# Reading the second attention's operands during the middle stage, and the gate chain in another order

## The chip, the cores and the metric

One core of one Trainium2 chip runs the whole program. Times are microseconds of device time for one execution; the kernel before takes 1930.31 us (median of 3 runs, 1929.67 to 1931.03). The trace is of one profiled execution.

## The reference, cut to what matters

Two post-norm transformer layers over x of 2048 tokens by 128 features. Layer 0 is a causal attention of 16 heads of 64 and a gated feed-forward of width 512; layer 1 is an attention of 16 heads of 8 with a Gaussian bias on the scores, and a linear layer. What the change touches lies between the feed-forward of layer 0 and the attention of layer 1:

```python
mixed_q = x @ wq + bq;  mixed_k = x @ wk + bk;  mixed_v = x @ wv + bv
glo = mean(mixed_q, axis=1)                          # over all 2048 tokens
c = tanh(mixed_q @ wfq + bfq + (glo @ wfg + bfg))    # the gate
P = sigmoid(sum(c * up, -1)) * 2048;  Z = sigmoid(sum(c * uz, -1)) * 2048   # per head
G = -(j - P) ** 2 * 2.0 / Z ** 2                     # j: position of the key
scores = q @ k.T / sqrt(8) + G;  probs = softmax(scores);  ctx = probs @ v
```

## The kernel before, in words

The program is a row of blocks; a block ends when all its engines have reached its end. First comes attention 0 (to 879 us of the span), then the middle stage (to 1100.9 us), attention 1 (to about 1866 us), and the last products and norms.

**The middle stage** runs over four chunks (c = 0 to 3) of 512 tokens: norm 0, the feed-forward, norm 1, then the projections of layer 1's query (kind "q"), key ("k"), value ("v") and gate ("f"). A chunk's projections are worked in between the feed-forward of the next chunk, those of chunk 3 at the end, alone. All orders are written out by hand, one list for each engine: TensorE (PE), ScalarE (ACT), VectorE (DVE), GpSimd (POOL), and SyncE (SP), which issues the DMAs.

Attention 1 takes scores from one bf16 product, so q and k are split into three bf16 parts each: POOL splits q into `parts_q` (lines 955 to 961), DVE splits k into `parts_k` (1235 to 1238). SP writes them to DRAM as `q_rows` and `k_rows` (line 927), where a head has 48 rows (`R_A`): six pairings of a part of q with a part of k, of 8 features each. The bias G is a square in the key's position, so it becomes 12 more rows: six of the coefficient a, three of w1 and three of w0 (each coefficient split in three bf16 parts; a's parts stand twice). Against them stand rows of constants in `krows`.

**The gate chain** at the end of the stage is: q of chunk 3 (ACT `mq`, 1121), DVE's mean `glo`, PE's `wfg` product (1075), DVE's `cbias` (1283), ACT's tanh of all four chunks from `cpre` into `cgate` (1165), PE's 64 narrow products (1082) that sum c over a head's features with `up` and `uz` into two banks of PSUM, `ps_g0` (for P) and `ps_g1` (for Z), ACT's two sigmoids (1169), and DVE's arithmetic: reciprocal `rz` (1288), `na` (1289), `uu` (1292), `f1` (1295), `f0` (1298). ACT and DVE then split these three into `parts_a`, `parts_w1`, `parts_w0` (1172, 1175, 1305), and SP writes them to `g_rows` (line 937), a first (six DMAs), then w1 and w0 (three each). The block ends when all of it has landed.

**Attention 1** works in 16 units u: four groups of four heads, by four chunks of 512 queries. SP reads a unit's operands into one of three slots of `qrows` (`load_q`, 1407 and 1409: four copies of 48 and four of 12 rows) and a group's keys into one of two slots of `krows` (`load_k`, 1414). The first unit's operands are read at the block's start. A unit's maxima come first (PE products 1478 into `ps_x` and `ps_y`, DVE maxima 1574 and 1578, 64 blocks of 512 keys); they run a unit ahead of its scores (1514), exponentials (ACT 1453) and weighted values (1524). SP puts the maxima into `qrows` too (`place_max`, 1432), and reads unit u + 2 when the scores of unit u - 1 are done.

Of the kernel before, what the change touches and what calls it, by code (L numbers as in the profile page):

```python
# [14 lines left out]
P = 128  # L15
# [125 lines left out]
def build(nc, a, out):  # L141
# [643 lines left out]
    GR = R_M - R_A  # L785
# [5 lines left out]
    gd = nc.dram_tensor("g_rows", (GR, NC, H1, S), BF16, kind="Internal").ap()  # L791
# [3 lines left out]
    krows = l1.enter_context(nc.sbuf_tensor("krows", [P, 2, HG, HALF], BF16))  # L795

    with ExitStack() as ctx:
# [11 lines left out]
        act_b = sb("act_b", [P, NH, QC])  # L809
# [16 lines left out]
        parts = {n: sb(f"parts_{n}", [P, 3, S], BF16) for n in "qk"}  # L826
        cpre = sb("cpre", [P, S - QC])
# [6 lines left out]
        cbias = sb("cbias", [P, 1])  # L834
        sig = sb("sig", [P, 2, JB])
# [20 lines left out]
        s_bl = sem("s_bl")  # L856
        s_tp = sem("s_tp")
# [25 lines left out]
        s_dr = sem("s_dr")  # L883

# [18 lines left out]
        def _(sp):  # L903
# [19 lines left out]
            for c in range(NQ):  # L923
                for n, dst, split_done, order in (("q", qd, s_pq, Q_PART), ("k", kd, s_pk, K_PART)):
                    sp.wait_ge(split_done, c + 1)
                    for m, part in enumerate(order):
                        sp.dma_start(dst[:, D1 * m:D1 * m + D1, CHUNK[c]], parts[n][:, part, CHUNK[c]]).then_inc(s_dr, 16)
                        n_d += 1
            for n, row, rep in (("a", 0, 2), ("w1", 6, 1), ("w0", 9, 1)):
                for i in range(3):  # L930
# [4 lines left out]
                    for r in range(rep):  # L935
                        src = gparts[n][:, i] if n != "a" else gparts[n][:, i].to_broadcast([P, NC, JB])
                        sp.dma_start(gd[row + rep * i + r].rearrange("c h (j s) -> (h j) c s", s=JB), src).then_inc(s_dr, 16)
                        n_d += 1
            sp.wait_ge(s_dr, 16 * n_d)

        @block.gpsimd
        def _(pool):
# [10 lines left out]
            for c in range(NQ):  # L953
                pool.wait_ge(s_qs, c + 1)
                pool.tensor_copy(parts["q"][:, 0, CHUNK[c]], qs[:, c % 2]).then_inc(s_pd, 1)
                pool.wait_ge(s_pd, 3 * c + 1)
                pool.tensor_tensor(qs[:, c % 2], qs[:, c % 2], parts["q"][:, 0, CHUNK[c]], ALU.subtract).then_inc(s_pd, 1)
                pool.wait_ge(s_pd, 3 * c + 2)
                pool.tensor_copy(parts["q"][:, 1, CHUNK[c]], qs[:, c % 2]).then_inc(s_pd, 1)
                pool.wait_ge(s_pd, 3 * c + 3)  # L960
                pool.tensor_tensor(parts["q"][:, 2, CHUNK[c]], qs[:, c % 2], parts["q"][:, 1, CHUNK[c]], ALU.subtract)\
# [3 lines left out]
        def _(pe):  # L965
# [106 lines left out]
            for kind in "qfkv":  # L1072
                project(kind, c)
# [692 lines left out]
```

## Time and profile before

| | before |
|---|---|
| median of 3 runs | 1930.31 us |
| the profiled execution | 1929.04 us |
| its span, first to last instruction | 1927.2 us |
| PE, DVE, ACT, POOL busy, share of span | 86%, 69%, 50%, 31% |
| mean granted TensorE clock, share of 2.4 GHz | 0.957 |
| DMA, mean over the span | 20 GB/s |

The profiled execution is 1.84 us longer than its span, and 1.27 us below the median. Shares are averages over stages with different limits, so they do not tell what a change between two stages is worth; that is read from the stretch between 1060 and 1115 us. The page's own chain of what ended last covers only the last norm, so the chain here is followed engine by engine.

### The profile page before, as it was taken

Reading aid. Unit: us, or ns where it says so; the run is one execution under the profiler, and the core shown is the slowest. Engines: PE = TensorE matmul, PEld = TensorE weight load, DVE = VectorE, ACT = ScalarE, POOL = GpSimd, SP = SyncE. Lnnn points to the kernel's source line nnn. Section 1 sums busy time; section 2 is a strip of 40 time slices with the busy share of each in tenths; the row PEclk is TensorE's granted clock in tenths of the full one; section 3 lists DMA queues with packets and bytes.
Section 4 is the critical chain, followed back from the end, with each engine's and each line's share of the span. In section 5 each row is a group of like instructions: output and inputs, shape, how many; then the busy total and the mean of one; then the engine's idle time right before and its main releaser. Section 6 shows DMA issues by size and latency. Waiting matters only on the chain. (4 is left out here: it accounts for less than half of the span.)

```text
span 1927.2 us, 27492 instructions
## 1 busy us (share of the span) xinstructions
PE 1651.8 (86%) x10672; PEld 529.6 (27%) x10672; DVE 1333.2 (69%) x2289; ACT 968.9 (50%) x1116; POOL 596.4 (31%) x325
## 2 busy tenths in 40 slices
PE   7899999999999999997999358888888888888863
PEld 3233333333333333323444201111111111111121
DVE  5767676767667676743333388888888888888716
ACT  3344444444444444442443206777777777777760
POOL 1576757667676767780000000000000000000000
PEclk9999999999999999997999658999999999999995
DMA  5000000000000000001011440112111211111000
GB/s 126 1 2 1 2 1 2 2 1 2 1 2 1 2 1 2 2 1 18 14 52 33 122 71 1 28 36 37 24 22 22 38 22 22 22 22 23 2 2 25
DMA packets 58420, 39.04 MB, mean 20 GB/s; under 512 B 20238, under 2 KB 55602, under 8 KB 58290
## 3 DMA queue, kind: packets, MB, share of 16 engines
q1 hardware_dynamic: 57474, 37.08, 9.2%
q8 instruction: 85, 1.39, 0.3%
q14 instruction: 45, 0.37, 0.1%
q10 hardware_dynamic: 816, 0.20, 0.0%
HBM read 25.53 MB, written 10.49 MB: 19 GB/s over the span
## 5 line engine op out<-in xcount | busy, mean ns | idle before, releaser
L1453 ACT ACTIVATE probs<-ps_e 128x1024 f32<-128x1024 f32 x512 | 498.6, 1022 | 256.1 <-PE ps_e L1514 254.7
L393 POOL TENSOR_TENSOR acc<-acc,probs 128x1024 f32<-128x1024 f32 (+3 forms) x256 | 502.7, 1964 | 210.2 <-DVE probs L754 139.0
L424 ACT ACTIVATE probs<-ps_e 128x1024 f32<-128x1024 f32 (+1 forms) x320 | 288.4, 901 | 375.1 <-PE ps_e L563 242.5
L1574 DVE TENSOR_REDUCE maxpart<-ps_x 128x2 f32<-128x1024 f32 x351 | 428.1, 1220 | 68.0 <-PE ps_x L1478 65.2
L582 PE MATMUL ps_o<-probs,v 128*64 128x512 f32 (+3 forms) x1280 | 307.6, 558 | 14.1 <-DVE probs L754 11.1
L1524 PE MATMUL ps_o<-probs,v 128*9 128x512 f32 x2048 | 269.2, 598 | 46.1 <-ACT probs L1453 30.4
L674 DVE TENSOR_REDUCE maxpart<-ps_x 128x2 f32<-128x1024 f32 x192 | 233.9, 1218 | 56.8 <-PE ps_x L492 54.0
L1478 PE MATMUL ps_x<-krows,qrows 60*128 60x512 bf16 x702 | 152.7, 402 | 102.2 <-DVE maxpart L1574 70.6
L1578 DVE TENSOR_REDUCE maxpart<-ps_y 128x1 f32<-128x512 f32 x322 | 220.4, 684 | 18.8 <-PE ps_y L1478 15.9
L1514 PE MATMUL ps_e<-qrows,krows 62*128 62x512 bf16 x1024 | 220.1, 383 | 10.2 <-DMA qrows<-maxrow 5.9
L677 DVE CUSTOM_DVE_ANT_0 masked<-ps_x,later 128x128 f32<-128x128 f32 (+3 forms) x256 | 115.2, 487 | 65.2 <-PE ps_x L492 64.0
L1478 PE MATMUL ps_y<-krows,qrows 60*128 60x512 bf16 x322 | 129.2, 401 | 7.8
L492 PE MATMUL ps_x<-k_hi,q_hi 64*128 64x512 f16 (+3 forms) x640 | 112.2, 347 | 14.5 <-DVE maxpart L674 11.4
L545 PE MATMUL ps_e<-q_hi,k_hi 64*128 64x512 f16 (+3 forms) x640 | 115.2, 357 | 1.3 <-DMA mrow<-maxrow 1.3
L545 PE MATMUL ps_e<-q_lo,k_hi 64*128 64x512 f16 (+3 forms) x640 | 112.0, 346 | 0.0
L545 PE MATMUL ps_e<-q_hi,k_lo 64*128 64x512 f16 (+3 forms) x640 | 111.9, 346 | 0.0
L1478 PEld LDWEIGHTS ps_x<-krows,qrows 60*128 60x128 bf16 x702 | 36.3, 94 | 260.1 <-DVE maxpart L1574 211.3
L388 POOL TENSOR_TENSOR acc<-probs 128x1024 f32<-128x1024 f32 x32 | 75.3, 2352 | 78.6 <-ACT probs L424 41.7
L582 PEld LDWEIGHTS ps_o<-probs,v 128*64 128x64 f32 x1280 | 65.0, 135 | 100.8 <-issue 88.1
L754 DVE TENSOR_TENSOR probs<-probs,keep 128x256 f32<-128x256 f32 (+1 forms) x128 | 83.1, 652 | 12.1 <-ACT probs L424 12.1
L1514 PEld LDWEIGHTS ps_e<-qrows,krows 62*128 62x128 bf16 x1024 | 59.1, 95 | 104.1 <-ACT probs L1453 73.8
L545 PEld LDWEIGHTS ps_e<-q_hi,k_hi 64*128 64x128 f16 x640 | 30.7, 93 | 157.1 <-issue 107.9
(251 smaller groups left out, 1476.8 us busy)
## 6 DMA issues: line engine op xcount, KB each, us to landing
qrows<-q_rows SPq DMA_DIRECT2D x64, 192.0 KB
q_rows<-parts_q SPq DMA_DIRECT2D x24, 128.0 KB, 2.4
k_rows<-parts_k SPq DMA_DIRECT2D x24, 128.0 KB, 2.4
krows<-k_rows SPq DMA_DIRECT2D x8, 384.0 KB, 7.8
qrows<-g_rows SPq DMA_DIRECT2D x64, 48.0 KB
raw_h<-in_L_ffn_h_w SPq DMA_DIRECT2D x2, 1024.0 KB, 6.7
mrow<-maxrow SPq DMA_DIRECT2D x128, 2.0 KB
g_rows<-parts_a SPq DMA_DIRECT2D x6, 256.0 KB, 2.7
```

Of the source, the lines that this page charges most:

```text
L393: pool.tensor_tensor(acc[:, u % 2, :, o:], acc[:, u % 2, :, o:], probs[:, turn % RING, :, o:], ALU.add)\
L424: act.activation(probs[:, turn % RING, :, o:], ps_e[:, turn % 2, :, o:], ACT.Exp, scale=1.0 / math.sqrt(D0))\
L545: mm = pe.matmul(out[:, h, o:], k_part["k"][rows, p % 2, keys], q_part["q"][rows, p % 2, queries], start=n == 0 and turn % 2 == 0, stop=n ...
L582: mm = pe.matmul(ps_o[D0 * h:D0 * h + D0, o:], v[:, p % 2, kt, D0 * h:D0 * h + D0], probs[:, turn % RING, h, o:], start=kt == 0, stop=kt = ...
L674: dve.reduce_max(maxpart[:, u % 2, :, t, c:c + 1], ps_x[:, :, 0:w], AX.X).then_inc(s_xf, 1)
L677: ins = dve.tensor_tensor_reduce(out=masked[:, h, 0:w], in0=ps_x[:, h, 0:w], in1=later[:, QC - w:QC], scale=1.0, scalar=-3e38, op0=ALU.add ...
L1453: act.activation(probs[:, HG * (turn % 2) + hh], ps_e[:, e % 2], ACT.Exp).then_inc(s_ex, 1)
L1478: return pe.matmul(out, qrows[64 * j:64 * j + R_M, u % 3, c, hh, t * P:(t + 1) * P], krows[64 * j:64 * j + R_M, u // NQ % 2, hh, c * KB:(c ...
L1514: mm = pe.matmul(ps_e[:, e % 2, j], krows[64 * j:64 * j + R_END, u // NQ % 2, hh, at * P:(at + 1) * P], qrows[64 * j:64 * j + R_END, u % 3 ...
L1524: mm = pe.matmul(ps_o[32 * hh:32 * hh + D1 + 1, :], v1[:, TU * j + at, HG * (u // NQ) + hh, :], probs[:, HG * (turn % 2) + hh, j, :], star ...
L1574: dve.reduce_max(maxpart[:, at:at + op[2]], ps_x[:, 0:op[2], :], AX.X).then_inc(s_xf, 1)
L1578: dve.reduce_max(maxpart[:, at:at + 1], ps_y[:, :], AX.X).then_inc(s_yf, 1)
```

## The change

1. **The reads move.** `qrows`, its semaphores and `load_q`, `load_k` are now made before the middle stage. SP reads group 0's keys there, a chunk at a time (`load_k_chunk`), and q of units 0 and 1, each one chunk after it was written; only the coefficient rows of unit 0 (`load_g`) come after the last write, still inside the block. Attention 1's block begins with `load_g(1)`.
2. **The rows of a.** They stand once in DRAM (`a_rows`), not four times. `load_q` and `load_g` are apart, so a unit takes 12 DMAs, not 8.
3. **The writes of the coefficients** go by part, then by coefficient, and wait only for the parts they need.
4. **The gate chain.** PE does the gate's last projection and the `wfg` product ahead of k and v of chunk 3; ACT loads the tanh table with a one-column `warm` tanh, and takes the four tanhs ahead of k. The 64 narrow products are done for `ps_g1` first, and then for `ps_g0`, with a signal after each.
5. **Room.** `parts_q`, `parts_k` hold two chunks and no more four, so their writers wait for the DMA of two chunks ago; `cpre` is gone (tanh works in place in `cgate`); `act_b` lies in `x_sb`.

```diff
...
-    gd = nc.dram_tensor("g_rows", (GR, NC, H1, S), BF16, kind="Internal").ap()
+    ga = nc.dram_tensor("a_rows", (R_W1 - R_A, H1, S), BF16, kind="Internal").ap()
+    gd = nc.dram_tensor("w_rows", (R_M - R_W1, NC, H1, S), BF16, kind="Internal").ap()
...
+    qrows = l1.enter_context(nc.sbuf_tensor("qrows", [P, 3, 2, HG, QC], BF16))
...
+    def load_k_chunk(eng, g, c):
+        j, at = divmod(c * QC, HALF)
+        eng.dma_start(krows[64 * j:64 * j + R_A, g % 2, :, at:at + QC],
+                      kd[HG * g:HG * g + HG, :, c * QC:(c + 1) * QC].rearrange("h r s -> r h s")).then_inc(s_k[g % 2], 16)
...
+    def load_k(eng, g):
+        for c in range(NQ):
+            load_k_chunk(eng, g, c)
...
+    def load_q(eng, u):
+        g, qc = divmod(u, NQ)
+        for j in range(2):
+            for c in range(2):
+                eng.dma_start(qrows[64 * j:64 * j + R_A, u % 3, c, :, :],
+                              qd[HG * g:HG * g + HG, :, qc * QC:(qc + 1) * QC].rearrange("h r s -> r h s"))\
+                    .then_inc(s_q[u % 3], 16)
+
+    def load_g(eng, u):
+        g, qc = divmod(u, NQ)
+        for j in range(2):
+            for c in range(2):
+                eng.dma_start(qrows[64 * j + R_A:64 * j + R_W1, u % 3, c, :, :],
+                              ga[:, HG * g:HG * g + HG, qc * QC:(qc + 1) * QC]).then_inc(s_q[u % 3], 16)
+                eng.dma_start(qrows[64 * j + R_W1:64 * j + R_M, u % 3, c, :, :],
+                              gd[:, 2 * j + c, HG * g:HG * g + HG, qc * QC:(qc + 1) * QC]).then_inc(s_q[u % 3], 16)
...
-        act_b = sb("act_b", [P, NH, QC])
+        act_b = x_sb[:, :, :].rearrange("p (i t) d -> p i (t d)", i=NH)
...
-        parts = {n: sb(f"parts_{n}", [P, 3, S], BF16) for n in "qk"}
-        cpre = sb("cpre", [P, S - QC])
+        parts = {n: sb(f"parts_{n}", [P, 2, 3, QC], BF16) for n in "qk"}
...
                 for n, dst, split_done, order in (("q", qd, s_pq, Q_PART), ("k", kd, s_pk, K_PART)):
                     sp.wait_ge(split_done, c + 1)
...
-                        sp.dma_start(dst[:, D1 * m:D1 * m + D1, CHUNK[c]], parts[n][:, part, CHUNK[c]]).then_inc(s_dr, 16)
-                        n_d += 1
-            for n, row, rep in (("a", 0, 2), ("w1", 6, 1), ("w0", 9, 1)):
-                for i in range(3):
+                        sp.dma_start(dst[:, D1 * m:D1 * m + D1, CHUNK[c]], parts[n][:, c % 2, part, :]).then_inc(s_dp[n][c], 16)
+                if c == 0:
+                    sp.wait_ge(s_dr, 16 * n_d)
+                else:
+                    sp.wait_ge(s_dp["q"][c - 1], 96)
+                    if c < NQ - 1:
+                        load_q(sp, c - 1)
+                    sp.wait_ge(s_dp["k"][c - 1], 96)
+                    load_k_chunk(sp, 0, c - 1)
+            n_d = 0
+            for i in range(3):
+                for n in ("a", "w1", "w0"):
                     if i < 2:
                         sp.wait_ge(s_hi[n], i + 1)
                     else:
                         sp.wait_ge(s_re[n], 2)
-                    for r in range(rep):
-                        src = gparts[n][:, i] if n != "a" else gparts[n][:, i].to_broadcast([P, NC, JB])
-                        sp.dma_start(gd[row + rep * i + r].rearrange("c h (j s) -> (h j) c s", s=JB), src).then_inc(s_dr, 16)
+                    if n == "a":
+                        for r in range(2):
+                            sp.dma_start(ga[2 * i + r].rearrange("h (j s) -> (h j) s", s=JB), gparts[n][:, i, 0]).then_inc(s_dg, 16)
+                            n_d += 1
+                    else:
+                        sp.dma_start(gd[(0 if n == "w1" else 3) + i].rearrange("c h (j s) -> (h j) c s", s=JB), gparts[n][:, i])\
+                            .then_inc(s_dg, 16)
                         n_d += 1
-            sp.wait_ge(s_dr, 16 * n_d)
+                if i == 0:
+                    sp.wait_ge(s_dp["k"][NQ - 1], 96)
+                    load_k_chunk(sp, 0, NQ - 1)
+                    sp.wait_ge(s_dp["q"][NQ - 1], 96)
+            sp.wait_ge(s_dg, 16 * n_d)
+            load_g(sp, 0)
...
-                pool.tensor_copy(parts["q"][:, 0, CHUNK[c]], qs[:, c % 2]).then_inc(s_pd, 1)
+                if c >= 2:
+                    pool.wait_ge(s_dp["q"][c - 2], 96)
+                pool.tensor_copy(parts["q"][:, c % 2, 0], qs[:, c % 2]).then_inc(s_pd, 1)
...
             c = NQ - 1
             to_tokens("n1", c)
             to_features("n1", c)
-            for kind in "qfkv":
-                project(kind, c)
+            project("q", c)
+            project("f", c)
             pe.wait_ge(s_gl, 1)
             pe.matmul(ps_j[:, 0:1], w1["wfg"][:, :], glo[:, :], start=True, stop=True).then_inc(s_gp, 1)
+            project("k", c)
+            project("v", c)
             pe.wait_ge(s_bl, 2)
-            for j in range(NJ):
-                if j % 2 == 0:
-                    pe.wait_ge(s_ca, j // 2 + 1)
-                for m in range(2):
+            for m in (1, 0):
+                for j in range(NJ):
+                    if m == 1 and j % 2 == 0:
+                        pe.wait_ge(s_ca, j // 2 + 1)
                     for t in range(4):
                         mm = pe.matmul(ps_g[m][32 * t:32 * t + 32, 0:JB],
                                        slide[:, m, t, NJ - 1 - j:5 * NJ - 1 - j],
                                        cgate[:, j * JB:(j + 1) * JB], start=j == 0, stop=j == NJ - 1,
                                        skip_group_check=True)
-            mm.then_inc(s_pp, 1)
+                mm.then_inc(s_pp, 1)
...
-                    act.activation(cpre[:, CHUNK[c]], j_bank(kind, c)[:, :], ACT.Copy).then_inc(s_jf, 1)
+                    act.activation(cgate[:, CHUNK[c]], j_bank(kind, c)[:, :], ACT.Copy).then_inc(s_jf, 1)
...
             projected("q", c)
-            projected("k", c)
+            act.wait_ge(s_fb, 1)
+            act.activation(warm[:, :], fbias[:, :], ACT.Tanh)
             act.wait_ge(s_jf, J_AT["f", c - 1] + 1)
             act.wait_ge(s_cb, 1)
             for c in range(NQ):
                 if c == NQ - 1:
                     act.wait_ge(s_jp, J_AT["f", c] + 1)
-                act.activation(cgate[:, CHUNK[c]], cpre[:, CHUNK[c]] if c < NQ - 1 else j_bank("f", c)[:, :], ACT.Tanh,
+                act.activation(cgate[:, CHUNK[c]], cgate[:, CHUNK[c]] if c < NQ - 1 else j_bank("f", c)[:, :], ACT.Tanh,
                                bias=cbias[:, 0:1]).then_inc(s_ca, 1)
-            act.wait_ge(s_pp, 1)
+            projected("k", c)
             for m in (1, 0):
+                act.wait_ge(s_pp, 2 - m)
                 act.activation(sig[:, m], ps_g[m][:, 0:JB], ACT.Sigmoid).then_inc(s_sg, 1)
...
-            link(dve.tensor_tensor(fbias[:, :], col["bfg"][:, :], col["bfq"][:, :], ALU.add))
+            dve.tensor_tensor(fbias[:, :], col["bfg"][:, :], col["bfq"][:, :], ALU.add).then_inc(s_fb, 1)
+            dve.wait_ge(s_fb, 1)
...
-            load_k(sp, 0)
-            load_q(sp, 0)
-            load_q(sp, 1)
+            load_g(sp, 1)
             load_q(sp, 2)
+            load_g(sp, 2)
             load_k(sp, 1)
...
                 if 1 <= u and u + 2 < NU:
                     load_q(sp, u + 2)
+                    load_g(sp, u + 2)
...
```

PE at the end of the middle stage, before: `l_wq`, `l_wk`, `l_wv` are the projections of chunk 3, `l_wfq` the gate's, `l_wfg` the product with the mean.

```order
L1037 MATMUL ps_h<-xt,l_wq 128x512
L1035 MATMUL ps_h<-mq,l_wfq 128x512
L1037 MATMUL ps_u<-xt,l_wk 128x512
L1032 MATMUL ps_u<-l_wv,xt 128x128 x4
L1075 MATMUL ps_j<-glo,l_wfg 128x1
L1082 MATMUL ps_g<-cgate,slide 32x256 x64
```

The same place now:

```order
L1088 MATMUL ps_h<-xt,l_wq 128x512
L1086 MATMUL ps_h<-mq,l_wfq 128x512
L1126 MATMUL ps_j<-glo,l_wfg 128x1
L1088 MATMUL ps_u<-xt,l_wk 128x512
L1083 MATMUL ps_u<-l_wv,xt 128x128 x4
L1135 MATMUL ps_g<-cgate,slide 32x256 x64
```

The product with the mean moved from behind k and v to ahead of both. The two halves of the narrow products read alike in this listing; now all 32 of `ps_g1` stand ahead of the 32 of `ps_g0`, where four of each took turns.

ACT at the same place, before:

```order
L1121 ACTIVATE mq<-ps_h,l_bq 128x512
L1125 ACTIVATE mk<-ps_u,l_bk 128x512
L1165 ACT_TABLE_LOAD
L1165 ACTIVATE cgate<-cpre,cbias 128x512 x3
L1165 ACTIVATE cgate<-ps_h,cbias 128x512
L1169 ACT_TABLE_LOAD
L1169 ACTIVATE sig<-ps_g 128x256 x2
```

And now:

```order
L1174 ACTIVATE mq<-ps_h,l_bq 128x512
L1213 ACT_TABLE_LOAD
L1213 ACTIVATE warm<-fbias 128x1
L1219 ACTIVATE cgate<-cgate,cbias 128x512 x3
L1219 ACTIVATE cgate<-ps_h,cbias 128x512
L1178 ACTIVATE mk<-ps_u,l_bk 128x512
L1224 ACT_TABLE_LOAD
L1224 ACTIVATE sig<-ps_g 128x256 x2
```

The table load and the four tanhs moved ahead of `mk`, the copy of k; the `warm` tanh is new.

SP at the end of the middle stage and into attention 1, before:

```order
L927 DMA q_rows<-parts_q 16x8x512 x6
L927 DMA k_rows<-parts_k 16x8x512 x6
L937 DMA g_rows<-parts_a 128x4x256 x6
L937 DMA g_rows<-parts_w 128x4x256 x6
L797 UNCONDITIONAL_BRANCH
L1420 UNCONDITIONAL_BRANCH
L1414 DMA krows<-k_rows 48x4x1024 x2
```

Now, first the end of the stage (the listing joins w1 and w0):

```order
L802 DMA krows<-k_rows 48x4x512
L959 DMA q_rows<-parts_q 16x8x512 x6
L959 DMA k_rows<-parts_k 16x8x512 x6
L802 DMA krows<-k_rows 48x4x512
L977 DMA a_rows<-parts_a 128x256 x2
L980 DMA w_rows<-parts_w 128x4x256 x2
L802 DMA krows<-k_rows 48x4x512
L977 DMA a_rows<-parts_a 128x256 x2
L980 DMA w_rows<-parts_w 128x4x256 x2
L977 DMA a_rows<-parts_a 128x256 x2
L980 DMA w_rows<-parts_w 128x4x256 x2
L821 DMA qrows<-a_rows 6x4x512
```

and the turn to the next block, where the first three rows are the last of unit 0's eight:

```order
L823 DMA qrows<-w_rows 6x4x512
L821 DMA qrows<-a_rows 6x4x512
L823 DMA qrows<-w_rows 6x4x512
L826 UNCONDITIONAL_BRANCH
L1458 UNCONDITIONAL_BRANCH
L821 DMA qrows<-a_rows 6x4x512
L823 DMA qrows<-w_rows 6x4x512
L821 DMA qrows<-a_rows 6x4x512
```

The reads of `q_rows` and `k_rows` for the first unit are gone from the block's start (those of q stand two chunks further up in the list), the writes of a and w take turns, and `load_g(0)` is ahead of the block's end.

## Rows read from the trace of the kernel before

**Rows 1.** Waits, 1050 to 1125 us: who waited for what, total, times, longest.

```profile
PE ps_x L1478 <- DMA qrows<-g_rows: 31.5, 1, 31.5
```

**Rows 2.** Timeline of SP, 1046 to 1125 us: start, duration, instruction, count.

```profile
1074.36 5.21 SPq L927 DMA_DIRECT2D k_rows<-parts_k  x6
1085.59 6.89 SPq L937 DMA_DIRECT2D g_rows<-parts_a  x6
1092.52 5.11 SPq L937 DMA_DIRECT2D g_rows<-parts_w  x6
1100.86 0.82 SPq L1414 DMA_DIRECT2D krows<-k_rows  x2
...
1104.74 0.40 SPq L1409 DMA_DIRECT2D qrows<-g_rows  x1
```

**Rows 3.** Waits of SP's queue, whole span.

```profile
SPq L1432 <- DVE maxrow L1583: 584.2, 15, 45.0
SPq L927 <- POOL parts_q L961: 140.1, 4, 51.5
...
SPq L797 <- DMA g_rows<-parts_w: 2.8, 1, 2.8
```

**Rows 4.** DMA issues: count, KB each, median us from issue to landing.

```profile
k_rows<-parts_k SPq DMA_DIRECT2D x24, 128.0 KB, 2.4
...
qrows<-g_rows SPq DMA_DIRECT2D x64, 48.0 KB
...
g_rows<-parts_w SPq DMA_DIRECT2D x6, 256.0 KB, 3.7
```

**Rows 5.** Timeline of PE, 1046 to 1125 us; in brackets idle before, and releaser.

```profile
1065.74 2.08 PE L1035 MATMUL ps_h<-mq,l_wfq 128*128 128x512 f32 x2 [0.78 <-ACT mq L1121]
1067.61 1.91 PE L1037 MATMUL ps_u<-xt,l_wk 128*128 128x512 f32 x2
...
1070.91 0.28 PE L1075 MATMUL ps_j<-glo,l_wfg 128*128 128x1 f32 x2
1073.63 8.80 PE L1082 MATMUL ps_g<-cgate,slide 128*32 128x256 f32 x128 [2.44 <-ACT cgate L1165]
1113.96 0.61 PE L1478 MATMUL ps_x<-krows,qrows 60*128 60x512 bf16 x2 [31.53 <-DMA qrows<-g_rows]
```

**Rows 6.** Timeline of ACT, same stretch.

```profile
1069.56 0.69 ACT L1125 ACTIVATE mk<-ps_u,l_bk 128x512 f32<-128x512 f32 x1 [3.87 <-PE ps_u L1037]
1071.47 1.28 ACT L1165 ACT_TABLE_LOAD   x1 [1.22 <-DVE cbias L1283]
1072.76 1.95 ACT L1165 ACTIVATE cgate<-cpre,cbias 128x512 f32<-128x512 f32 x3
...
1082.49 0.66 ACT L1169 ACTIVATE sig<-ps_g 128x256 f32<-128x256 f32 x2 [5.90 <-PE ps_g L1082]
```

**Rows 7.** Timeline of DVE, same stretch.

```profile
1073.67 0.88 DVE L1244 TENSOR_TENSOR v<-ps_u,l_bv 128x128 f32<-128x128 f32 x4
1082.90 1.75 DVE L1288 RECIPROCAL rz<-sig 128x256 f32<-128x256 f32 x1 [8.35 <-ACT sig L1169]
...
1087.22 1.22 DVE L1298 SCALAR_TENSOR_TENSOR f<-f,uu 128x1024 f32<-128x1024 f32 x1
...
1091.42 2.35 DVE L1305 TENSOR_TENSOR parts_w<-f,parts_w 128x1024 bf16<-128x1024 f32 x2
```

**Rows 8.** Line 1082 by windows: PE and weight loads busy, granted clock, DMA share, GB/s.

```profile
1073.60:1074.60 1.00, 0.97 (x16) 0.76 (x20) 0.80 0.74 197
1074.60:1077.40 2.80, 2.80 (x33) 1.68 (x27) 0.50 0.76 207
1077.40:1082.50 5.10, 5.03 (x92) 3.33 (x84) 0.98 0.33 88
```

**Rows 9.** PE by windows in attention 1: busy, granted clock, DMA share, GB/s.

```profile
1157.00:1172.00 15.00, 12.71 (x48) 0.50 0.01 3
1172.00:1204.00 32.00, 26.49 (x189) 0.98 0.00 1
```

More of the change, by code:

```diff
@@ L795, in build @@
     krows = l1.enter_context(nc.sbuf_tensor("krows", [P, 2, HG, HALF], BF16))
+    qrows = l1.enter_context(nc.sbuf_tensor("qrows", [P, 3, 2, HG, QC], BF16))
+    s_q = [l1.enter_context(nc.semaphore(f"s_q{b}")) for b in range(3)]
+    s_k = [l1.enter_context(nc.semaphore(f"s_k{b}")) for b in range(2)]
+    def load_k_chunk(eng, g, c):
[20 more added lines that the diff above has]
+                              gd[:, 2 * j + c, HG * g:HG * g + HG, qc * QC:(qc + 1) * QC]).then_inc(s_q[u % 3], 16)
     with ExitStack() as ctx:
@@ L834, in build @@
         cbias = sb("cbias", [P, 1])
+        warm = sb("warm", [P, 1])
         sig = sb("sig", [P, 2, JB])
@@ L856, in build @@
         s_bl = sem("s_bl")
+        s_fb = sem("s_fb")
         s_tp = sem("s_tp")
@@ L883, in build @@
         s_dr = sem("s_dr")
+        s_dg = sem("s_dg")
+        s_dp = {n: [sem(f"s_dp_{n}{c}") for c in range(NQ)] for n in "qk"}
         T_USES = [("n0", 0)]
@@ L1233, in key @@
                 dve.wait_ge(s_jf, J_FREE["k", c] + 1)
-                src, dst = mk[:, c % 2], parts["k"]
-                link(dve.tensor_copy(dst[:, 0, CHUNK[c]], src))
-                link(dve.tensor_tensor(rest[:, :], src, dst[:, 0, CHUNK[c]], ALU.subtract))
-                link(dve.tensor_copy(dst[:, 1, CHUNK[c]], rest[:, :]))
-                dve.tensor_tensor(dst[:, 2, CHUNK[c]], rest[:, :], dst[:, 1, CHUNK[c]], ALU.subtract).then_inc(s_pk, 1)
+                src, dst = mk[:, c % 2], parts["k"][:, c % 2]
+                if c >= 2:
+                    dve.wait_ge(s_dp["k"][c - 2], 96)
+                link(dve.tensor_copy(dst[:, 0], src))
+                link(dve.tensor_tensor(rest[:, :], src, dst[:, 0], ALU.subtract))
+                link(dve.tensor_copy(dst[:, 1], rest[:, :]))
+                dve.tensor_tensor(dst[:, 2], rest[:, :], dst[:, 1], ALU.subtract).then_inc(s_pk, 1)
                 dve.wait_ge(s_pk, c + 1)
@@ L1323, in build @@
         SLOTS = 2 * HG
-        qrows = sb("qrows", [P, 3, 2, HG, QC], BF16)
         probs = sb("probs1", [P, SLOTS, 2, QC], F32)
@@ L1338, in build @@
         ps_yb = ps_y[:, :].bitcast(BF16)
-        s_q = [sem(f"s_q{b}") for b in range(3)]
-        s_k = [sem(f"s_k{b}") for b in range(2)]
         s_mrd = [sem(f"s_mrd1{b}") for b in range(2)]
@@ L1399, in build @@
                         (X_DONE if op[0] == "x" else Y_DONE)[b // BU] = op[3] + 1
-        def load_q(eng, u):
-            g, qc = divmod(u, NQ)
-            cols = slice(qc * QC, (qc + 1) * QC)
-            heads = slice(HG * g, HG * g + HG)
-            for j in range(2):
-                for c in range(2):
-                    eng.dma_start(qrows[64 * j:64 * j + R_A, u % 3, c, :, :],
-                                  qd[heads, :, cols].rearrange("h r s -> r h s")).then_inc(s_q[u % 3], 16)
-                    eng.dma_start(qrows[64 * j + R_A:64 * j + R_M, u % 3, c, :, :],
-                                  gd[:, 2 * j + c, heads, cols]).then_inc(s_q[u % 3], 16)
-        def load_k(eng, g):
-            for j in range(2):
-                eng.dma_start(krows[64 * j:64 * j + R_A, g % 2],
-                              kd[HG * g:HG * g + HG, :, HALF * j:HALF * j + HALF].rearrange("h r s -> r h s"))\
-                    .then_inc(s_k[g % 2], 16)
         block = ctx.enter_context(nc.Block())
@@ L1475, in max_block @@
                 if n == 0:
[L1476 to L1477 removed]
+                    pe.wait_ge(s_q[u % 3], 192 * (u // 3 + 1))
+                    pe.wait_ge(s_k[u // NQ % 2], 16 * NQ * (u // NQ // 2 + 1))
                 return pe.matmul(out, qrows[64 * j:64 * j + R_M, u % 3, c, hh, t * P:(t + 1) * P],
```

9 lines of the change are left out of this document (3 added, 6 removed).

## The prediction

> **What bounds the kernel here.** I read three views in this order: who waited for whom around the change, the timelines of SP and PE there, and then ACT and DVE backwards from the last write. The reader is to see one long wait. PE sits idle for 31.5 us, from the end of the narrow gate products at 1082.4 to the first product of attention 1 at 1113.96, and it is released by a DMA into `qrows` [rows 1, 5]. No other engine does anything for the result from 1093.8 on, when DVE has the last coefficient part [rows 7]. So all that shortens this stretch shortens the span, one for one: behind it stand DVE's maxima, which start with PE's first product. The wait has three pieces, each with its own limit.
> - The chain that makes the coefficients. It starts at the product with the mean, which ends at 1071.2 because k and v stand ahead of it, although f ended at 1067.8 [rows 5]. Then come 0.2 for `cbias`, a table load of 1.28 and four tanhs [rows 6], 8.8 us of narrow products [rows 5], and DVE's arithmetic, with `f0` ready at 1088.44 and the last part at 1093.77 [rows 7].
> - The writes. SP issues them from 1085.59 to 1097.63 [rows 2], and the last has landed 2.8 us after that, at 1100.4 [rows 3]. That is 12 x 256 KB = 3072 KB in 14.8 us, 207 KB/us: late by volume, not by data, which was there 3.9 us before the last issue ended.
> - The reads. SP issues keys and unit 0's q and coefficients from 1100.86 on. Unit 0's last issue starts at 1104.74, and PE starts 9.2 us later [rows 2, 5]: by size two key halves of 384 KB, 768 KB of q and 192 KB of coefficients [rows 4], 1728 KB in 13.1 us, 132 KB/us.
>
> **The chain, worked forward.** Times are of the profiled execution. f still ends at 1067.8 on PE. The product with the mean takes 0.28 and needs the mean, which has been waiting by then, so it ends at 1068.1 and `cbias` is there at 1068.3, where it was 1071.4. The tanh table is loaded by `warm` behind `mq`, at 1065.7 plus 1.28, so by 1067.3 with the small tanh: hidden behind PE's f. The tanhs run from 1068.4, three in 1.95 and one in 0.67, to 1071.0. k and v, on PE, come after the product with the mean: 0.3 later than before, to 1071.3. So the narrow products start at 1071.3 with all of `cgate` there, and the bound has moved from the tanhs to PE itself. They started at 1073.63 [rows 5].
>
> How long they take depends on the clock. Before, they ran at the full level from 1077.4 on, 92 records in 5.1 us, and at half from 1074.6 to 1077.4, 33 records in 2.8 us [rows 8]. That is 18 and 11.8 records/us, so the 128 take 7.1 us at full and 10.8 at half; 8.8 was the mix. The drop at 1074.6 came after PE had been idle for 2.44 us. Now no such gap is left, PE is busy from 1065.7 through to the end, so I take 7.1 and keep 10.8 as the other end. The Trainium skill (TensorE: Matmul & The Clock Gate, "HAM oscillation — how this bites in real kernels") says that work which follows a wait starts throttled, and that grouping work without waits keeps the clock up. This row's drop agrees; by the rule the sum is the one below, and without it, with 8.8 as measured, the gain would be 1.7 smaller.
>
> The half for Z is done after 3.55 us, at 1074.9. The sigmoid's table load (the 1.28 again) sits behind `mk`: tanhs to 1071.0, `mk` 0.69, load to 1073.0, hidden. If that cover were gone it would cost up to 1.3. The reciprocal started 0.4 after the sigmoids did [rows 6, 7], so now at 1075.3. DVE must be free by then: it splits k and adds v first, 3.2 us from 1071.4 to 1074.55 before [rows 6, 7], now from `mk` at 1071.7 to 1074.9. Just free. 1.75 brings 1077.05, `na` is ready at 1077.5. The half for P is done at 1078.4, its sigmoid's arithmetic starts about 1078.9, and `uu`, `f1` and `f0` need what they needed before: from the sigmoid pair's second end at 1083.15 [rows 6], with the reciprocal in between (to 1084.65), `uu` began at 1085.0 and `f0` was done 3.4 later. So 1082.3, which is 6.1 earlier than 1088.44. The last part follows 5.33 after `f0` as before: 1087.6.
>
> **The writes.** k's rows of chunk 3 still end at about 1079.6 (5.21 us of issue [rows 2]; its data are as late as before). Then SP has one key chunk, the two DMAs of a's first part, and w1's first at about 1082.1, when ACT has it. w0's first goes at 1083.4, 1.1 after `f0`. From there SP is the limit: that issue, one key chunk, four of a (mean of the row 1.15, but that was with 256 KB each behind a full queue; I take 0.45, the issue of the small ones [rows 2]) and four of w at 0.85 (5.11 over six [rows 2]), about 6.9 with gaps. Last issue done at 1090.3, landed 2.8 later, 1093.1. By volume: 1536 KB of w, 384 of a and a key chunk of 192 at 207 KB/us is 10.2 us from 1081, 1091.2, so volume no longer limits. Before it was 1100.4: 7.3 earlier, of which 6.1 is the chain.
>
> **The reads.** Eight issues at 0.45 (0.40 and a gap [rows 2]): the last starts at 1096.3. Its landing is not in the trace of before. The bounds are 2.4, a DMA into an almost empty queue [rows 4], and 9.2, the wait above with 1728 KB under way. 192 KB is far nearer to the first, so I take 2.4: 1098.7. The block's end and DVE's clearing of `ps_o` (before, 0.8 behind the block's start) lie beside that landing. PE starts at 1098.8, not 1113.96: 15.2 us earlier, 6.1 by the chain, 1.2 by the writes, 7.9 by the reads.
>
> **At nothing.** The reads moved into the middle stage: 4 q issues of 0.4 and a key chunk for each of two chunks, where SP waits tens of us for POOL's next q (140 us in four waits [rows 3]). If that cover were gone, two chunks' worth would be 4 us on SP, still behind data. The waits of POOL and DVE for DMAs of two chunks ago are for transfers that landed 2.4 us after issue [rows 4], a chunk earlier; behind DVE's wait stand k's split and v, and none of it waits. In attention 1 the four more issues of each unit are 1.8 us of SP, which waits 584 us for maxima over 15 units [rows 3]; `load_g(1)` and the rest put 24 issues, 11 us, ahead of the first `place_max`, which waits for 64 blocks of DVE's maxima anyway. The narrower parts, `cgate` in place and `act_b` in `x_sb` change addresses only.
>
> **Rivals.**
> A. The narrow products run at half clock, although there is no gap. Then `f0` comes 3.7 later and all behind it: gain 11.5, 1918.8. For it: PE was at half until 1077.4 while busy [rows 8].
> B. The small reads land late. Each goes to six rows of `qrows`, where one of before went to twelve. If a DMA used only as many of the 16 engines as it has rows, six would carry 192 KB; at 132/16 = 8.25 KB/us each that is 3.9 us, as long as the issues, and at half of that rate 7.8, the last landing 4.2 later: gain 11.0, 1919.3. Against: nothing else is in the queues. The Trainium skill has that rule (DMA: Bandwidth & Descriptors, "Why a DMA increments its semaphore by 16 and not by 1": the engines used divide the slowest dimension, here 6); no row here tells the engines of one DMA.
> C. SP stays behind: the 5.21 us for k's rows is a queue already full, and the key chunks put between prolong it, so the writes end as volume did before. Then the chain's 6.1 is lost and 9 are left: 1921.3.
> D. Nothing to measure: another wait of the same length takes over at the block's start. PE, ACT and DVE show none but the DMA [rows 1]. Under 3.9 us of gain.
> E. Slower. Attention 1 starts at the low clock, which held until 1172, in work with 48 records in 15 us against 189 in 32 us at full [rows 9]: 3.2 and 5.9 per us. If the shorter pause left the clock low for longer, each us would lose 0.46 of PE's work; it must last 33 us beyond 1172's counterpart to eat 15.2, and at 60 us it is 12 slower, 1942. For it: the clock stayed low for all of 1157 to 1172 with PE busy 12.7 of 15. Against: it came back then, without any change in the work's kind, and PE has spare time in a unit.
>
> **How the numbers follow.** The profiled execution would be 1929.04 - 15.2 = 1913.8; the median stands 1.27 above it, so 1915.1. Its own range, gains of 13 to 18: 1912 to 1917. Chances: forecast 0.78, A 0.07, B 0.06, C 0.04, D 0.03, E 0.02. The range goes down to 1911.5 (writes landing after 2.4 and issues at 0.35) and up to 1920.5, over A and B. About 0.2%, 3.9 us, is what a measurement can tell from no change. Faster 0.95, within 0.03, slower 0.02.
>
> **What would show it.** `cbias` near 1068.3; narrow products from 1071.3 for 7 us at full clock; the reciprocal near 1075.3; the last write landed near 1093; the last read of the block issued near 1096.3; PE's first product of attention 1 near 1098.8, and a unit's length in attention 1 unchanged. I am wrong if the first product waits past 1101 or the units become longer.

## The result, and the profile after

The changed kernel takes 1911.72 us (median of 4 runs, 1911.10 to 1911.87) against 1929.99 (4 runs) for the kernel before: ratio 0.9904, 95% interval 0.9887 to 0.9921. That is 18.3 us where 15.2 were forecast. The direction and the mechanism held; the size is a fifth over. The time lies below the 1912 to 1917 that the forecast gave itself, and just inside the low end of the wide range (1911.5).

| | before | after |
|---|---|---|
| profiled execution, span | 1929.04, 1927.2 | 1911.10, 1909.4 |
| PE, DVE, ACT busy | 86%, 69%, 50% | 86%, 70%, 51% |
| mean granted clock | 0.957 | 0.959 |
| PE idle ahead of attention 1 | 31.53 | 17.36 |

Timeline of PE in the changed kernel (start, duration; in brackets idle before), for [rows 5]:

```profile
1068.02 2.08 PE L1086 MATMUL ps_h<-mq,l_wfq 128*128 128x512 f32 x2 [0.78 <-ACT mq L1174]
1069.89 0.42 PE L1126 MATMUL ps_j<-glo,l_wfg 128*128 128x1 f32 x2
...
1073.53 7.11 PE L1135 MATMUL ps_g<-cgate,slide 128*32 128x256 f32 x128
1098.01 0.61 PE L1516 MATMUL ps_x<-krows,qrows 60*128 60x512 bf16 x2 [17.36 <-DMA qrows<-w_rows]
```

Everything ahead of the change ran 2.28 us later in this execution (the gate's last projection starts at 1068.02, before at 1065.74), so I count from the start of that projection, below called f. The product with the mean follows f at once, and the narrow products take 7.11, where they took 8.80.

Timelines of ACT and DVE, for [rows 6, 7]:

```profile
1070.61 1.95 ACT L1219 ACTIVATE cgate<-cgate,cbias 128x512 f32<-128x512 f32 x3 [1.12 <-DVE cbias L1341]
...
1077.26 0.38 ACT L1224 ACTIVATE sig<-ps_g 128x256 f32<-128x256 f32 x1 [2.26 <-PE ps_g L1135]
```

```profile
1077.68 1.75 DVE L1346 RECIPROCAL rz<-sig 128x256 f32<-128x256 f32 x1 [0.69 <-ACT sig L1224]
...
1081.13 0.90 DVE L1350 TENSOR_SCALAR uu<-sig 128x256 f32<-128x256 f32 x4 [1.24 <-ACT sig L1224]
...
1083.32 1.23 DVE L1356 SCALAR_TENSOR_TENSOR f<-f,uu 128x1024 f32<-128x1024 f32 x1
...
1087.53 2.35 DVE L1363 TENSOR_TENSOR parts_w<-f,parts_w 128x1024 bf16<-128x1024 f32 x2
```

The tanh table is there when `cbias` comes, and Z's sigmoid runs 3.4 us ahead of P's: `uu` waits for P's sigmoid and no more for the reciprocal.

Timeline of SP, for [rows 2]:

```profile
1084.40 1.62 SPq L980 DMA_DIRECT2D w_rows<-parts_w  x2
...
1087.63 1.13 SPq L980 DMA_DIRECT2D w_rows<-parts_w  x2
1087.63 0.46 SPq L980 DMA_DIRECT2D w_rows<-parts_w  x1
1088.39 0.37 SPq L980 DMA_DIRECT2D w_rows<-parts_w  x1
1088.81 1.44 SPq L977 DMA_DIRECT2D a_rows<-parts_a  x2
1090.29 1.04 SPq L980 DMA_DIRECT2D w_rows<-parts_w  x2
1093.62 0.29 SPq L821 DMA_DIRECT2D qrows<-a_rows  x1
...
1096.00 0.30 SPq L823 DMA_DIRECT2D qrows<-w_rows  x1
```

The third and fourth row are the second taken apart: its 1.13 holds a pause of 0.30 for w0's second part. One issue of w takes 0.37 to 0.55 here, where five of the six of before took 0.85 to 0.88; each read takes 0.30. DMA issues (count, KB each, median us to landing), for [rows 4]:

```profile
w_rows<-parts_w SPq DMA_DIRECT2D x6, 256.0 KB, 2.6
...
a_rows<-parts_a SPq DMA_DIRECT2D x6, 64.0 KB, 2.6
```

The whole stretch, step by step, counted from f:

| step | before | forecast | after |
|---|---|---|---|
| `cbias` starts | 5.49 | 2.4 | 2.33 |
| narrow products start, take | 7.89, 8.80 | 5.6, 7.1 | 5.51, 7.11 |
| `f0` done | 22.70 | 16.6 | 16.53 |
| last coefficient part done | 28.03 | 21.9 | 21.86 |
| last write issued | 31.89 | 24.6 | 23.31 |
| SP goes on with the reads | 35.12 | 27.4 | 25.60 |
| last read unit 0 needs starts | 39.00 | 30.6 | 27.98 |
| PE's first product of attention 1 | 48.22 | 33.1 | 29.99 |

The stretch is 18.23 shorter. The rest of the span is 0.4 longer (2.3 longer up to f, 1.9 shorter from attention 1 on): 17.8 in the spans.

### The profile page after: what moved, and what is told of

Same layout as the page of the kernel before. It is cut to its first block and busy times, and to the rows that moved or that the text cites. A ratio compares the mean times of both kernels' runs of the same rounds, so it can differ in the third digit from the quotient of the medians.

```text
span 1909.4 us, 27571 instructions
## 1 busy us (share of the span) xinstructions
PE 1650.9 (86%) x10672; PEld 529.0 (28%) x10672; DVE 1333.6 (70%) x2289; ACT 969.3 (51%) x1117; POOL 596.3 (31%) x325
## 5 line engine op out<-in xcount | busy, mean ns | idle before, releaser
L754 DVE TENSOR_TENSOR probs<-probs,keep 128x256 f32<-128x256 f32 (+1 forms) x128 | 83.9, 658 | 12.1 <-ACT probs L424 12.1
```

## The experiments

The measure is the stretch from f to PE's first product of attention 1: 48.22 before, 29.99 after, and 47.47 and 30.44 when both were profiled once more. So a difference under 0.8 us in it is not to be leaned on. It falls into two parts. From f to the last coefficient part it is 28.03 and 21.86, and 26.69 and 22.32 once more: this part moves with the clock. Behind the last part it is 20.19 and 20.78 in the two profiles of before, and 8.12 in both of after; small effects on writes and reads are better read there. Whole times of one kernel spread over up to 6 us in these runs, and serve as a check only.

### The chain alone

```diff
# before, with:
-            for kind in "qfkv":
-                project(kind, c)
+            project("q", c)
+            project("f", c)
...
+            project("k", c)
+            project("v", c)
...
+            act.activation(warm[:, :], fbias[:, :], ACT.Tanh)
...
+                act.wait_ge(s_pp, 2 - m)
```

> The kernel before with the gate chain of the change alone (order of PE and ACT, the warm tanh, Z's half of the narrow products first); reads and writes as before. I measure the stretch from the start of the gate's last projection on PE to PE's first product of attention 1: 48.2 us before, 30.0 after the change. Theory (the pieces add up): the last coefficient part is ready 6.2 us earlier, the writes start 6.2 earlier and keep their 14.8 us by volume, so the stretch is 42.0 and the time 1923.8. Rival (the queue still holds k's rows when the writes start): the writes start earlier but end only 2 to 4 us earlier, stretch 44 to 46, time 1926 to 1928.

Measured: stretch 43.03, 5.19 less than before; 1924.39 us, ratio 0.9969 (0.9956 to 0.9981). Timeline of SP, this kernel:

```profile
1082.58 7.16 SPq L939 DMA_DIRECT2D g_rows<-parts_a  x6
1089.79 5.10 SPq L939 DMA_DIRECT2D g_rows<-parts_w  x6
1098.14 0.82 SPq L1421 DMA_DIRECT2D krows<-k_rows  x2
```

f is at 1068.89 here. The writes start 6.2 earlier against f (13.7, was 19.85), the reads 5.9 earlier (29.25, was 35.12), and 0.7 of that is lost in the reads, a part no one touched. The stretch, 43.03, lies halfway between the theory's 42.0 and the rival's 44; what tells them apart is the writes, whose issues end 5.9 earlier, where the rival had 2 to 4. The 0.7 is no effect of the edit: from the first read to PE it is 13.78 here, 13.70 in the kernel before once more, and 13.10 in its first profile.

### The reads and writes alone

```diff
# after, with the order of PE and ACT of before
-            project("q", c)
-            project("f", c)
+            for kind in "qfkv":
+                project(kind, c)
...
-            act.activation(warm[:, :], fbias[:, :], ACT.Tanh)
```

> The changed kernel with the gate chain of before: reads in the middle stage, a's rows once, writes by part. Theory: the last part is ready 28.0 us after the start of the gate's last projection, as before, and what follows takes the 8.1 us that it takes in the changed kernel (1.45 to the end of the last issue, 2.3 to landing, 2.4 to the last read's issue, 2.0 to PE): stretch 36.2, 12 us less than before, time 1918. Rival (with late data the writes bunch up again): 38 to 40, time 1920 to 1922.

Measured: stretch 36.18, 12.04 less than before; 1916.98 us, ratio 0.9929 (0.9917 to 0.9942). Timeline of SP:

```profile
1094.05 1.04 SPq L980 DMA_DIRECT2D w_rows<-parts_w  x2
1097.38 0.29 SPq L821 DMA_DIRECT2D qrows<-a_rows  x1
```

With f at 1065.57 the last part is done at 28.04, the last write issued at 29.52 and the reads go on at 31.81: the 8.1 us behind the last part are the same, whatever the chain. The theory holds to the tenth. Against the first profile of before, the two edits alone are worth 5.2 and 12.0, both together 18.2. That the sum is 1.0 short is not shown to be anything but the spread of the part behind the last part in the old form (20.19 to 20.88 in three profiles).

### a's rows four times again

```diff
-    ga = nc.dram_tensor("a_rows", (R_W1 - R_A, H1, S), BF16, kind="Internal").ap()
+    ga = nc.dram_tensor("a_rows", (R_W1 - R_A, NC, H1, S), BF16, kind="Internal").ap()
...
-                            sp.dma_start(ga[2 * i + r].rearrange("h (j s) -> (h j) s", s=JB), gparts[n][:, i, 0]).then_inc(s_dg, 16)
+                            sp.dma_start(ga[2 * i + r].rearrange("c h (j s) -> (h j) c s", s=JB), gparts[n][:, i].to_broadcast([P, NC, JB])).then_inc(s_dg, 16)
```

> The changed kernel, but a's rows are written four times to DRAM, as before (six DMAs of 256 KB and no more 64 KB); each read takes its own copy. Theory (the writes of before were late by volume, and the 0.85 us for an issue was a full queue): 1152 KB more at 207 KB/us, so the last write lands about 4 us later, issues of w take 0.8 us again; stretch 34, time 4 us above the changed kernel. Rival (the writes are bound by SP's issues and the last part): no difference.

Measured: stretch 32.05, 2.1 over the changed kernel (2.0 of it behind the last part); 1914.18 us. Timeline of SP, this kernel:

```profile
1088.71 1.38 SPq L980 DMA_DIRECT2D w_rows<-parts_w  x2
1090.13 1.98 SPq L977 DMA_DIRECT2D a_rows<-parts_a  x2
1092.15 1.79 SPq L980 DMA_DIRECT2D w_rows<-parts_w  x2
1096.63 0.28 SPq L821 DMA_DIRECT2D qrows<-a_rows  x1
```

The same two pairs of writes of w take 1.38 and 1.79, not 1.13 and 1.04; one by one 0.66 to 0.88, not 0.37 to 0.55. They land 3.6 us after issue, not 2.6. So the duration of an issue is not a price of the instruction: it grows with what the queue already holds. But 1152 KB cost 2.1 us and not 4, so 207 KB/us was no limit of the queue. The windows of the kernel before show it (engines' busy times, then granted clock, DMA share, GB/s at the end of a row):

```profile
1085.00:1089.00 4.00, 0.00 (x0) 0.00 (x0) 3.90 (x9) 2.00 (x3) 0.00 (x0) 0.86 0.46 131
1089.00:1093.00 4.00, 0.00 (x0) 0.00 (x0) 4.00 (x5) 2.95 (x4) 0.00 (x0) 0.50 0.56 156
1093.00:1097.00 4.00, 0.00 (x0) 0.00 (x0) 0.78 (x1) 0.00 (x0) 0.00 (x0) 0.50 1.02 288
1097.00:1100.50 3.50, 0.00 (x0) 0.00 (x0) 0.00 (x0) 0.00 (x0) 0.00 (x0) 0.50 0.86 242
```

While SP was waiting for data the DMAs moved 131 and 156 GB/s, and 288 and 242 once they were behind. My 207 was the mean of both. In the last two rows the DMA engines are busy for 1.02 and 0.86 of the time: only there was before late by volume.

### The writes by coefficient

```diff
-            for i in range(3):
-                for n in ("a", "w1", "w0"):
+            for n in ("a", "w1", "w0"):
+                for i in range(3):
```

> The changed kernel, but the writes go by coefficient again: all three parts of a, then w1, then w0. Theory (order matters since SP's queue is in order): the first write of w waits for a's third part, at 1087.6, and 1536 KB then go in one piece, to about 1096: stretch 32.5 to 33, 2.5 to 3 us above the changed kernel. Rival (the last part at 1089.9 sets the end whatever the order): under 0.5 us.

Measured: stretch 32.60, 2.6 over the changed kernel, all of it behind the last part (10.74 against 8.12); 1914.01 us. Timeline of SP:

```profile
1081.51 6.79 SPq L977 DMA_DIRECT2D a_rows<-parts_a  x6
...
1088.87 4.58 SPq L980 DMA_DIRECT2D w_rows<-parts_w  x6
1096.16 0.29 SPq L821 DMA_DIRECT2D qrows<-a_rows  x1
```

SP stands at a's parts until 1088.3, with w's first ready since about 1084, and then has six large writes in one piece. The theory holds: of the change's gain the order alone is 2.6.

### No warm tanh; the last reads behind the block's end

```diff
# the first kernel
-            act.wait_ge(s_fb, 1)
-            act.activation(warm[:, :], fbias[:, :], ACT.Tanh)
# the second kernel
-            load_g(sp, 0)            # end of the middle stage
+            load_g(sp, 0)            # first in attention 1
```

> The changed kernel without the warm tanh, so the tanh table is loaded on the chain. Theory (PE is behind k and v until 1073.5, and the tanhs have 1.3 us of slack for each chunk): no difference, under 0.3 us. Rival (the table load is on the path): 1.3 us more.

> The changed kernel, but unit 0's coefficient rows are read at the start of attention 1's block and no more at the end of the middle stage. Theory: only the block's end is put between the last landing and the first issue, 0.5 us as before; stretch 30.5. Rival (the block's start costs more, DVE's clearing and the first instructions now come behind it): 1.5 us or more.

Measured: without the warm tanh the stretch is 29.83 (1910.55 us), so the table load costs nothing where it was: DVE's reciprocal starts 0.5 later, at 10.17 from f and not 9.66, but `f0` is done at 16.46, as P's half sets it. With the reads behind the block's end it is 30.59 (1911.93 us), 0.6 more, 0.4 of it between the last write's issue and the first read (2.69 against 2.29); behind the last part it is 0.5 more. Both theories hold.

### v of chunk 3 last

```diff
             project("k", c)
-            project("v", c)
             pe.wait_ge(s_bl, 2)
...
                 mm.then_inc(s_pp, 1)
+            project("v", c)
...
             key(c)
-            value(c)
...
+            value(NQ - 1)            # DVE, behind the last part
```

> The changed kernel with v of chunk 3 projected after the narrow products on PE, and added on DVE after the last part. In the changed kernel PE reaches the narrow products 1.3 to 1.6 us after the first tanh chunk is ready, because of v. Theory: they start 1.5 us earlier (PE now meets the tanhs as they come), DVE's reciprocal follows right on its split of k, and all behind it moves by 1.5: stretch 28.5, time 1.5 under the changed kernel. Rival (waits for the tanhs between the products, or the clock falling with them): no gain, or up to 3 us lost.

Measured: stretch 29.57, 0.4 less and not 1.5; 1912.99 us (1908.74 to 1913.76). The narrow products on PE, and the same line by windows (PE and weight loads busy with counts, granted clock, DMA share, GB/s):

```profile
1074.11 8.08 PE L1134 MATMUL ps_g<-cgate,slide 128*32 128x256 f32 x128
```

```profile
1074.00:1075.00 1.00, 0.89 (x12) 0.44 (x16) 0.50 0.00 0
1075.00:1076.00 1.00, 1.00 (x16) 0.54 (x12) 0.50 0.02 5
1076.00:1077.00 1.00, 1.00 (x24) 0.49 (x18) 0.94 0.73 182
```

They start 4.14 after f, 1.4 earlier, but at half clock, and take 8.08. The clock rises at about 1076, 6.1 us after f; in the changed kernel it rose at about 1073 (5 after f), before they began. What was started earlier ran at the low level, so the P half ended only 0.4 earlier. The rival was nearer, by another way than it said: the clock did not fall, it had not yet risen. A part of that is this execution's and not the edit's: the changed kernel profiled once more also had the rise 6.1 after f, and against that profile v last gains 0.87 and not 0.4. The part behind the last part is 8.1 in all three.

### Two queues, and the last landing

```diff
# two queues (v last as well)
+            act.wait_ge(s_re["w0"], 2)
+            act.dma_start(gd[5]..., gparts["w0"][:, 2]).then_inc(s_dg, 16)
+            act.wait_ge(s_dg, 16 * 12)
+            load_g(act, 0, (1,))
# a's reads first (v last as well)
-                if i == 0:
                     sp.wait_ge(s_dp["k"][NQ - 1], 96)
                     load_k_chunk(sp, 0, NQ - 1)     # now behind the writes
+            sp.wait_ge(s_da, 96)
+            load_g(sp, 0, w_rows=False)
+            sp.wait_ge(s_dg, 96)
+            load_g(sp, 0, a_rows=False)
```

> As the kernel with v last, and the last write of w0's third part and half of unit 0's coefficient reads are issued by ACT. Theory (the end of the stage is bound by SP's issues one after the other): the last write is issued 0.5 us earlier, the reads take four issues of 0.34 in place of eight, 1.3 less: stretch 26.7, 3.3 us under the changed kernel. Rival (the landing times decide, or a second queue costs a start-up): only the 1.5 of v last, or less.

> v last as before, the last key chunk is read behind the coefficient writes, and a's rows are read as soon as a's writes have landed, ahead of the landing of w's. Theory (the end of the stage is SP's list and what its queue still has to move): w's last write is issued 0.5 to 0.8 us earlier, only four of eight reads stand behind the last landing (1.4 less): stretch 27.5 to 28, 2 us under the changed kernel's 30.0. Rival (a's reads and the key chunk put their own traffic among w's writes, which land that much later): 29 to 29.5, no gain over v last alone (29.6).

> The same, and ACT issues the last write of w0 and two of the four last reads. Theory (SP's issues still bound it): 0.5 for the write and 0.7 for the reads less than with SP alone, stretch 26.5 to 27. Rival (it is the landing of the writes and one round trip of the reads by now, as with the two queues before, where four reads fewer gave 0.5): at most 0.5 less than with SP alone.

The third kernel does both: SP reads a's rows first, and ACT issues w0's last write and two of the four last reads.

Measured: stretches 29.05, 29.23 and 29.36 (1910.11, 1910.46 and 1910.60 us; ratios to before 0.9894, 0.9899 and 0.9897, with intervals of about 0.0015 to either side). Two queues, SP and ACT:

```profile
1091.86 0.44 SPq L983 DMA_DIRECT2D w_rows<-parts_w  x1
1095.20 0.28 SPq L821 DMA_DIRECT2D qrows<-a_rows  x1
```

```profile
1091.46 0.38 ACTq L1235 DMA_DIRECT2D w_rows<-parts_w  x1
```

ACT issues w0's last write at 1091.46, but SP is with w1's until 1092.30, and the reads go on at 1095.20. a's reads first, SP and PE:

```profile
1091.24 1.04 SPq L983 DMA_DIRECT2D w_rows<-parts_w  x2
...
1092.97 1.62 SPq L822 DMA_DIRECT2D qrows<-a_rows  x4
1094.99 1.29 SPq L825 DMA_DIRECT2D qrows<-w_rows  x4
```

```profile
1098.89 0.61 PE L1520 MATMUL ps_x<-krows,qrows 60*128 60x512 bf16 x2 [15.78 <-DMA qrows<-w_rows]
```

a's reads are out of the way by 1094.6 and only four stand behind the landing of w, which is at 25.3 from f, as in the kernel with v last (25.2). Yet PE starts 3.9 us after the first of these four, where the changed kernel needs 4.4 for all eight. So SP's list is no longer what sets the end. Behind the last part it is 7.5 to 7.8 us in these three, 8.1 in the changed kernel. All three theories fail, and the rivals' numbers hold. What is left is not landings alone. In the changed kernel the DMA engines are still full (1088 us to the last issue's end, then to the first read):

```profile
1088.00:1091.30 3.30, 0.00 (x0) 0.00 (x0) 1.88 (x2) 0.36 (x1) 0.00 (x0) 0.50 0.99 267
1091.30:1093.60 2.30, 0.00 (x0) 0.00 (x0) 0.00 (x0) 0.00 (x0) 0.00 (x0) 0.50 0.81 227
```

With a's reads first the share is 1.01 from 1093 to 1094 and 0.94 from 1094 to 1095. So the volume of w's last writes is a second limit of the landing, next to the round trip; no run here thins it (a's rows four times, which thickened it, took 2.0 more), and which of the two counts for how much stays open. Why the four last reads land 2.9 us after the last is issued, and the eight of the changed kernel 2.0, is open. The 0.3 to 0.6 gained behind the last part are more than that part varies (8.03 to 8.14 in five profiles with the same writes and reads), but in whole times no version here is faster than the changed kernel by more than the measurement tells.

### Both kernels once more

> The kernel before once more, for its profile. Attention 0 took 879.6 us in the first profile and 881.7 to 882.7 in most of the others, with the same instructions. Theory (it varies between executions of one kernel): this profile can lie anywhere from 879 to 883, and the stretch between the stages is 48.2 again to 0.2. Rival (the length goes with the kernel): 879.5 again to 0.1.

> The changed kernel once more, for its profile. Theory: attention 0 anywhere from 879 to 883, the stretch 30.0 to 0.2. Rival: attention 0 at 881.8 to 0.1, so that the changed kernel pays 2.3 us there.

Measured: attention 0 ends at 880.76 and 882.40 (first profiles 879.55 and 881.82), the stretches are 47.47 and 30.44, spans 1925.1 and 1909.3. Both theories had the stretch to 0.2, and both fail: it is 0.75 shorter and 0.45 longer. The narrow products, and PE by windows (busy, granted clock, DMA share, GB/s), first before once more, then after once more:

```profile
1075.01 8.50 PE L1082 MATMUL ps_g<-cgate,slide 128*32 128x256 f32 x128 [2.43 <-ACT cgate L1165]
1071.00:1072.00 1.00, 1.00 (x8) 0.98 0.00 0
```

```profile
1075.50 7.23 PE L1135 MATMUL ps_g<-cgate,slide 128*32 128x256 f32 x128
1075.00:1076.00 1.00, 1.00 (x11) 0.61 0.26 54
```

In before once more (f at 1068.16) the clock was already full 2.9 after f, not 5.0 as in the first profile. So k and v ran faster, `cbias` started at 4.44 and not 5.49, and the last part was done at 26.69, not 28.03. In after once more (f at 1069.65) it rose 6.1 after f, not 5.1: the products started at 5.85 and took 7.23, and the last part was done at 22.32, not 21.86. In this pair the chain's gain up to the last part is 4.4, not 6.2, the stretch is 17.0 shorter, not 18.2, and the spans 15.8, not 17.8. What is gained behind the last part, 12.1 and 12.7, hardly moves.

One window of attention 0 on PE, 30 to 60 us (busy, granted clock, DMA share, GB/s), in the order before, before once more, after, after once more:

```profile
30.00:60.00 30.00, 26.59 (x173) 0.89 0.01 2
```

```profile
30.00:60.00 30.00, 26.18 (x162) 0.83 0.00 1
```

```profile
30.00:60.00 30.00, 26.62 (x164) 0.80 0.01 2
```

```profile
30.00:60.00 30.00, 26.27 (x161) 0.81 0.01 2
```

Neither rival holds to its 0.1: the kernel before is found at 879.6 and 880.8, the changed one at 881.8 and 882.4. Over all 14 profiles attention 0, the same in every kernel, ends between 879.4 and 882.7. The granted clock between 30 and 60 us goes with it: 0.89 in the two that end before 880, 0.77 to 0.83 in all others. The edits do not sort it: the reads and writes alone end it at 879.4, the chain alone at 882.1. What sets it in an execution stays open.

## Why the mechanism was right, and where the size was off

**What bounds it: right.** The wait ahead of attention 1 was the whole matter: 17.8 us in the spans, 18.23 in the stretch, and the rest went the other way.

**The chain: right at every step, in part by luck.** `cbias`, the start of the narrow products, their 7.1 at full clock, `f0`, the last part: none is off by more than 0.1 in the first profile. But f and k themselves ran at half clock (0.50 from 1063 to 1073 in the changed kernel), which the prediction did not look at, and the level rose 5.1 after f, only 0.4 ahead of the products. Once more it rose 6.1 after f, 0.3 behind their start. The Trainium skill (TensorE: Matmul & The Clock Gate, "HAM oscillation — how this bites in real kernels") has the low stretch follow the wait, and this trace agrees: no wait before the products, no low stretch in them, 7.11 against 8.80. All 14 profiles agree: the level falls again, within 0.6 us of the products' start, in the three that have the wait of 2.4 us there (both of before, and the reads and writes alone), and in no other. The kernel with v last shows the other end: there the level of f's own time still held when they began, wait or no wait.

**The writes and reads: the failed step.** For what stands behind the last part the sum gave 11.2 us; it took 8.12, in both profiles. That is the whole 3.1, and it lies in four mis-sized terms. The first is "four of w at 0.85 (5.11 over six [rows 2])": they took 0.37 to 0.55 each, 1.83 together and not 3.4, because the 0.85 was a full queue's pace. Before, a's writes of the same 256 KB, and w's first, were quick too; w's second was not (SP):

```profile
1089.87 0.36 SPq L937 DMA_DIRECT2D g_rows<-parts_a  x1
...
1092.52 0.54 SPq L937 DMA_DIRECT2D g_rows<-parts_w  x1
1093.11 0.88 SPq L937 DMA_DIRECT2D g_rows<-parts_w  x1
```

Four of a, on the other hand, took 2.27 and not 1.8 (the last 0.85 by itself), and w's issue at the start of the sum was shorter as well; with pauses, the last issue was done 1.25 earlier than forecast. The second term, "landed 2.8 later", is 2.3: 0.5. The prediction took the 1.15 of a for a full queue's number and replaced it. That reading was wrong: a's six issues took 0.36 to 0.54 each, and the row's 6.89 holds two waits for data. It left w, the row that did show the full queue, as it was. The kernel with a's rows four times brings both numbers back toward their old size (0.87 and 0.88 for the last two of w).

The third term is the reads' issues. Eight at 0.45 took 0.34 from start to start: 0.8. The 0.45 was read from copies of 12 rows and 48 KB, and these have 6 and 24 KB. The fourth is their landing, 2.0 and not 2.4: 0.5.

**At nothing: right.** Units of attention 1 take 44.27 as before, SP's 24 issues are done at 1105.8 and the first `place_max` is at 1141.9. The warm tanh was counted as cover for 1.28; it is worth nothing that can be measured (29.83 without it, 29.99 with it).

**Rivals.** A did not occur (7.11 at full clock). B: PE started 2.0 after the last small read's issue began, so narrower reads were not late. (What the Trainium skill says of the engines that a copy uses, in DMA: Bandwidth & Descriptors, "Why a DMA increments its semaphore by 16 and not by 1", is neither shown nor refuted by that; it had no price here.) C: k's rows ended at 1081.2, 13.2 after f where 13.8 was taken, and SP was on time. D and E: attention 1 started at half clock as before, and the level rose in its first unit as before; that unit, from its maxima to its end, took 47.42 after 48.45, and 45.9 in both of the second profiles.

## What to carry to other kernels

The duration of a DMA's issue, read in a place where transfers are late, is the queue's pace and not the instruction's: take it from a place with an empty queue before pricing a change that thins the traffic. And look at each issue by itself: a merged row holds the waits for data between them. Where the wait at a stage's turn is a chain of compute, write, landing, read, landing, read ahead what is ready early, and put the writes in the order in which their data come: here that was 12 us, against 4.4 to 6.2 for the chain itself. After that, a second issuing engine and finer splits brought 0.3 to 0.6 us, too little to see in the whole time.

## What the runs showed of the hardware that was not expected

- The level of TensorE's clock can take back most of an earlier start: 64 narrow products started 1.4 us earlier took 1.0 us longer, at half clock until 1076.
- The rise of the clock came 2.9 us after the same instruction in one execution of the kernel before and 5.0 in the other, and moved the end of the chain by 1.3 us.
- Stages that nobody changed vary: attention 0 ended anywhere in 3.3 us over the 14 profiles, with its granted clock between 30 and 60 us at 0.77 to 0.89, and the first unit of attention 1 took 48.45 and 45.9 us in the two profiles of before. Steps of 0.1 to 0.5 us are seen only in a part counted between two fixed instructions, and best in one that the clock does not touch.
- The price of an issue did not follow size or rows: 0.30 us for 6 rows and 24 KB in the changed kernel; before, 0.40 for 12 rows and 48 KB, and 0.35 beside it for 48 rows and 192 KB.
